# Transposing two operands by DMA instead of TensorE in a fused expert, scan, expert kernel

## The chip, the cores and the metric

One core of a Trainium2 chip runs the whole kernel. The time is the device time in microseconds (us) of that core for one execution, and what is given for a kernel is the median of its runs. The engines are TensorE (PE in the rows; PEld is its weight load), VectorE (DVE), ScalarE (ACT), GpSimd (POOL) and SyncE (SP). In this kernel SP only issues DMAs.

## The reference

Three layers run over x, 2 sequences of 2048 tokens by 1024 features. The first and the third are a feed-forward layer with 64 small experts of rank 16, of which each token takes four; the second is a selective scan over time with 16 states for each feature.

```python
def ffn(x, A, B, W, bias):
    vecs = einsum('arh,bsh->bsar', A, x)            # 64 experts x 16
    arrows = norm(vecs, axis=-1)
    _, idx = top_k(arrows, 4)
    routes = one_hot(idx, 64).sum(-2) / 4
    v = einsum('bsa,bsar->bsr', routes, vecs)
    delta = einsum('bsa,ajr,bsr->bsj', routes, B, v)
    return einsum('bsh,jh->bsj', x, W) + bias + delta

def scan(x, W_xproj, W_dt, b_dt, A_log, D_param):
    delta_r, B_mat, C_mat = split(einsum('btd,rd->btr', x, W_xproj))
    delta = softplus(einsum('btr,dr->btd', delta_r, W_dt) + b_dt)
    h = exp(delta * -exp(A_log)) * h + delta * B_mat * x     # step by step over t
    return sum(h * C_mat) + x * D_param

x = x + 0.5 * ffn(layernorm(x), ...)
x = x + scan(layernorm(x), ...)
x = x + 0.5 * ffn(layernorm(x), ...)
```

## The kernel before

**Units.** The 4096 tokens are 32 blocks of 128. Each block passes the feed-forward layer twice, so there are 64 *units* of work; a unit of kind 1 is a block's first pass, one of kind 2 its second. `plan` sets their order. The scan is cut into 256 *groups* of four 128x512 pieces (a group is 4 states of a feature tile over 512 tokens), and these groups, some five in a unit, are laid between the parts of units 5 to 57 (the *slots* of a unit). Units 0 to 4 and 58 to 63 have next to no scan work.

**Order.** There is no scheduler. Every engine has a function `unit(l, a, b)` written by hand; `a` is the current unit, `b` the next one, `l` the one before. Each engine goes through its own list in order and waits on semaphores. SP's list of DMAs is in order too: a wait for one DMA's source holds every later DMA back.

**One unit on TensorE** is, in this order: `base` (the product with W, 50 matmuls of 128x512 into `po`), between its parts the transposes and products of the scan's inputs (`scan_blocks`, `scan_products`, only behind a unit of kind 1), the transposes of the scan's result for a unit of kind 2 (`y_blocks`, f32, from `uT`, which is used as the landing place `auxy`), `z` (a matmul for the step sizes), then `routed_blocks` (16 transposes of the routed rows), `routed` (48 matmuls with B into `po`), with `norm_blocks` of the next unit between its last parts (8 f32 transposes of the normalised rows `xn`), and `experts` of the next unit (48 matmuls with A into `pv`). `states` sums scan pieces and lies in between.

**f16 pairs.** Each f32 operand is split into a high and a low f16 part. Products take high*high, high*low and low*high. `xT` and `uT` hold both parts of the transposed normalised rows and of the transposed routed rows.

**From experts to routed.** ScalarE squares `pv` into `sel` (`squares`), VectorE sums (`sums`), takes the four largest (`choose`) and writes the routed rows as f16 high and low part into the same `sel` (`gather`, L1004 and L1009, semaphore `s_u`). TensorE transposes them into PSUM (L553), ScalarE copies them into `uT` (`routed_copy`, L763), and `routed` may start.

**From normalising to experts.** VectorE takes mean and variance (`unit_stats`, L955 and L957), ScalarE refines the scale (`prepare`, nine tiny instructions) and writes `xn` (`normed`, L741), TensorE transposes in f32 into PSUM (L462), ScalarE copies the halves to the high part of `xT` (`high`, L746), VectorE subtracts for the low part (`low_part`, L978), and `experts` may start.

**The scan's feeding.** For each tile of 4 groups: `z` on TensorE (L615), softplus on ScalarE and VectorE (`magnitudes`, `softplus`, `delta`), a store to DRAM (`delta_out`, issued by ScalarE), and after it landed broadcasting loads on SP (`spread_inputs` L307, `spread_delta` L300). GpSimd multiplies with B (`times_b`, L425 and L430), ScalarE makes the decays (L825), VectorE scans (L1034), GpSimd multiplies with C (`times_c`, L438), TensorE sums (L628). `load_ranks` (L324) brings the ranks for eight `z`; before, it is issued with the first tile of the eight (`load_tile`). `store_tile` (L337) stores a finished tile.

## Time and profile before

| | |
|---|---|
| median of 3 runs | 3056.54 us (3044.06 to 3065.63) |
| the profiled execution's own time | 3055.02 us |
| its span, first to last instruction | 3053.2 us |
| granted TensorE clock, mean | 0.965 |
| busy | PE 90%, VectorE 75%, ScalarE 51%, GpSimd 77% |
| DMA | 340 MB, 111 GB/s mean |

The rows come from one profiled execution, 1.5 us under the median; the sums stand against 3055.0 us. Between span and own time lie 1.8 us. Times in rows are us from the start of the span. A timeline row gives start, duration, engine, line, operation, output and inputs, and in brackets the idle time of that engine just before and what ended it.

### The profile page before, as it was taken

The numbers are of one execution on the slowest core, as the hardware profiler recorded it, in microseconds if no ns is written. First come the engines' busy times: TensorE is split into PE (matmuls) and PEld (weight loads), VectorE is DVE, ScalarE is ACT, GpSimd is POOL, SyncE is SP. The second block draws the span as 40 slices with busy tenths as digits, with TensorE's granted clock in tenths as the row PEclk, the third lists the DMA queues.
The fourth block names the chain that finished last, engine by engine and source line by source line (L and its number), as shares of the span: only waits on it lengthen the run. The fifth ranks groups of instructions, "written<-read, shape, count | busy, mean of one in ns | idle before, by whom it ended". The sixth has DMA issues, their size and how long they took to land.

```text
span 3053.2 us, 41481 instructions
## 1 busy us (share of the span) xinstructions
PE 2742.9 (90%) x14592; PEld 1275.1 (42%) x14592; DVE 2289.5 (75%) x2915; ACT 1558.1 (51%) x2915; POOL 2348.7 (77%) x703
## 2 busy tenths in 40 slices
PE   5998998999899899889799898899889988988999
PEld 2554444444443344344344443444344433433444
DVE  8335888688778878887688787788787878888533
ACT  5335565565645456555546554554555545454321
POOL 2004998789889899898799798899898989889300
PEclk8999999999999999999999999999999999999999
DMA  5114432433344333433343234333343344333110
GB/s 196 44 44 135 124 119 92 135 120 120 112 135 133 110 110 106 145 105 105 119 150 118 86 109 140 129 98 125 118 137 99 110 130 129 118 114 111 49 42 35
DMA packets 174215, 340.05 MB, mean 111 GB/s; under 512 B 12979, under 2 KB 88883, under 8 KB 174006
## 3 DMA queue, kind: packets, MB, share of 16 engines
q1 hardware_dynamic: 157110, 303.83, 31.0%
q10 hardware_dynamic: 16896, 33.56, 3.6%
q8 instruction: 116, 1.90, 0.3%
q14 instruction: 93, 0.76, 0.1%
HBM read 234.05 MB, written 103.29 MB: 110 GB/s over the span
## 4 chain that ended last, share of the span: by engine, by line
PE 29%; DVE 23%; DMA 13%; ACT 9%; DVEq 9%; issue 7%; POOL 7%; SPq 1%; ACTq 1%; POOLq 0%
DVE mreg L1034 11%; PE po L470 9%; PE pv L470 7%; DMA delta_scratch<-mreg 6%; PE po L474 5%; PE pv L474 4%; ACT pA L825 3%; DMA yT_scratch<-mreg 3%; POOL mreg L430 3%; POOL mreg L438 3%; DVEq L1036 3%; DVE pv L1001 2%; DVE sel L1009 2%; DVEq L1000 1%; DVE sel L998 1%
## 5 line engine op out<-in xcount | busy, mean ns | idle before, releaser
L438 POOL TENSOR_TENSOR mreg<-mreg 128x2048 f32<-128x2048 f32 x256 | 1160.5, 4534 | 43.1 <-DVE hst L1037 42.7
L430 POOL TENSOR_TENSOR mreg<-mreg 128x1024 f32<-128x1024 f32 x340 | 794.8, 2361 | 349.5 <-DMA mreg<-delta_scratch 273.2
L825 ACT ACTIVATE pA<-mreg,nA 128x512 f32<-128x512 f32 x1024 | 696.4, 687 | 691.0 <-DVE mreg L1034 617.2
L1034 DVE TENSOR_TENSOR_SCAN mreg<-pA,hst,mreg 128x512 f32<-128x512 f32 x768 | 943.8, 1266 | 109.5 <-ACT pA L825 80.2
L470 PE MATMUL po<-wB,uT 128*128 128x512 f16 x2016 | 487.8, 392 | 44.2 <-ACT uT L763 44.1
L470 PE MATMUL po<-wW,xT 128*128 128x512 f16 x2016 | 464.4, 381 | 0.0
L470 PE MATMUL pv<-wA,xT 128*128 128x512 f16 x2016 | 458.6, 381 | 1.3 <-DVE xT L978 1.1
L425 POOL TENSOR_TENSOR mreg<-mreg 128x2048 f32<-128x2048 f32 x86 | 389.7, 4532 | 54.6 <-issue 54.6
L1034 DVE TENSOR_TENSOR_SCAN mreg<-pA,cst,mreg 128x512 f32<-128x512 f32 x256 | 314.9, 1267 | 38.8 <-ACT pA L825 35.5
L628 PE MATMUL py<-mreg,Em 128*32 128x512 f32 x2048 | 280.8, 621 | 63.1 <-DVE mreg L1046 34.1
L470 PEld LDWEIGHTS po<-wB,uT 128*128 128x128 f16 x2016 | 198.7, 101 | 287.6 <-ACT uT L763 51.8
L470 PEld LDWEIGHTS pv<-wA,xT 128*128 128x128 f16 x2016 | 193.6, 98 | 274.4 <-issue 36.2
L470 PEld LDWEIGHTS po<-wW,xT 128*128 128x128 f16 x2016 | 198.3, 98 | 235.3 <-issue 17.8
L474 PE MATMUL pv<-wA,xT 128*128 128x512 f16 x1008 | 241.8, 383 | 35.2 <-DVE xT L978 34.9
L982 DVE TENSOR_REDUCE n<-sel 128x32 f32<-128x512 f32 x128 | 87.3, 683 | 237.4 <-ACT sel L753 237.0
L474 PE MATMUL po<-wW,xT 128*128 128x512 f16 x1008 | 254.9, 399 | 0.0
L474 PE MATMUL po<-wB,uT 128*128 128x512 f16 x1008 | 238.1, 379 | 0.0
L1014 DVE SCALAR_TENSOR_TENSOR xin<-po,sc,xin 128x512 f32<-128x512 f32 x128 | 95.6, 747 | 158.8 <-PE po L474 154.8
L474 PEld LDWEIGHTS pv<-wA,xT 128*128 128x128 f16 x1008 | 97.3, 98 | 162.3 <-issue 51.1
L474 PEld LDWEIGHTS po<-wW,xT 128*128 128x128 f16 x1008 | 98.3, 102 | 152.1 <-issue 60.4
L753 ACT ACTIVATE sel<-pv 128x512 f32<-128x512 f32 x128 | 74.8, 585 | 168.7 <-PE pv L474 168.5
L474 PEld LDWEIGHTS po<-wB,uT 128*128 128x128 f16 x1008 | 98.6, 98 | 105.0
(128 smaller groups left out, 2745.0 us busy)
## 6 DMA issues: line engine op xcount, KB each, us to landing
mreg<-delta_scratch SPq DMA_DIRECT2D x256, 512.0 KB, 5.3
delta_scratch<-mreg ACTq DMA_DIRECT2D x128, 256.0 KB
xin<-x SPq DMA_DIRECT2D x32, 512.0 KB, 4.7
x_scratch<-xin SPq DMA_DIRECT2D x32, 512.0 KB, 7.2
xnT_scratch<-auxs SPq DMA_DIRECT2D x32, 512.0 KB, 2.7
mreg<-xnT_scratch SPq DMA_DIRECT2D x64, 256.0 KB, 4.2
mreg<-bc_scratch SPq DMA_DIRECT2D x64, 256.0 KB, 5.7
yT_scratch<-mreg SPq DMA_DIRECT2D x64, 256.0 KB, 6.7
```

The costliest lines, as they stand in the source:

```text
L425: pool.tensor_tensor(Hr[:, G % NH, :, :], u, b.broadcast_to([P, 4, CT]), ALU.mult).then_inc(s_bm, 2)
L430: pool.tensor_tensor(Hr[:, G % NH, 2 * h:2 * h + 2, :], u, b.broadcast_to([P, 2, CT]), ALU.mult).then_inc(s_bm, 1)
L438: pool.tensor_tensor(h, h, Cr[:, g, :].unsqueeze(1).broadcast_to([P, 4, CT]), ALU.mult).then_inc(s_cm, 1)
L470: last = nc.tensor.matmul(dst, lhs[:, 0, k, :], w[:, wb, k, nb * HF:(nb + 1) * HF], start=(first and k == 0 and wb == 0), stop=False)
L474: last = nc.tensor.matmul(dst, lhs[:, 1, k, :], w[:, 0, k, nb * HF:(nb + 1) * HF], start=False, stop=(stop and k == KD - 1))
L628: last = nc.tensor.matmul(py[32 * s:32 * s + 32, :], Em[:, :], Hr[:, G % NH, s, :], start=(g == 0), stop=(g == 3), tile_position=(0, 32 * s))
L753: nc.scalar.activation(sel[:, nb * HF:(nb + 1) * HF], pv[:, nb, :], ACT.Square).then_inc(s_sq, 1)
L825: nc.scalar.activation(pA[:, i % 2, :], Dr[:, 2 * (n % NPR) + i % 2, :], ACT.Exp, scale=nA[:, c:c + 1]).then_inc(s_dA, 1)
L982: V.tensor_reduce(n2[:, nb * NE // 2:(nb + 1) * NE // 2], sel3[:, nb * NE // 2:(nb + 1) * NE // 2, :], AX.X, ALU.add)
L1014: V.scalar_tensor_tensor(dst, po[:, nb, :], sc[:, 3:4], dst, ALU.mult, ALU.add).then_inc(s_res, 1)
L1034: V.tensor_tensor_scan(h, pA[:, i % 2, :], h, before, ALU.mult, ALU.add).then_inc(s_sc, 1)
L1036: dve.drain()
```

## The change

- TensorE no longer transposes the routed rows (`routed_blocks` is gone) nor the normalised rows (`norm_blocks` is gone). ScalarE's copies `routed_copy` and both half copies `high` from PSUM are gone, VectorE's two half subtractions too.
- ScalarE now rounds `xn` to f16 in token order into `sel` (`high`, one instruction of 128x1024), VectorE subtracts in one instruction of 128x1024 (`low_part`), both SBUF to SBUF.
- SP issues two DMA transposes of the routed rows (`turn`, `sel` to `uT`) and two of the normalised rows (`turn_rows`, `sel` to `xT`) in each unit, 128x1024 in f16 each, 256 KB. Each has a wait: for `s_u`; for `s_xhi`, `s_xlo`, and for the end of `base`, which still reads `xT` (`s_bd`, new). The first unit's `turn_rows` is issued by ScalarE.
- `sel` is used by both, so `high` waits for the routed rows' transposes to have landed.
- Places: `load_ranks` moves ahead by a part of a unit or more (`ranks_due`); `store_tile` stands ahead of the spreads; `z(a, 1)` comes one part of `routed` earlier, `states(a, 0)` one part of `base` later; `unit_stats` comes one scan later; `low_part` stands behind scan 12 as a whole; `delta(a, 1)` and `delta(a, 2)` are set among the last scans.

```diff
+        xh = sel[:, :].bitcast(f16).rearrange("p (c n) -> p c n", c=2)
...
+        def turn_rows(q, b):
+
+            for part in range(2):
+                q.wait_ge(s_xhi if part == 0 else s_xlo, b.u + 1)
+                if part == 0:
+                    q.wait_ge(s_bd, b.u)
+                q.dma_start_transpose(xT[:, part, :, :], xh[:, part, :]).then_inc(s_xT[part], 16)
...
+            def turn(a, y_done):
+
+                for part in range(2):
+                    sp.wait_ge(s_u, a.u * 2 + 1 + part)
+                    if part == 0:
+                        sp.wait_ge(s_yT, 2 * y_done)
+                    src = un2[:, part, :, :].rearrange("p k q -> p (k q)")
+                    sp.dma_start_transpose(uT[:, part, :, :], src).then_inc(s_uc[part], 16)
...
+            def ranks_due(a, pos):
+
+                if pos in a.zs and a.zs[pos] % KD == 0:
+                    load_ranks(a.zs[pos] // KD)
...
                 slot(a, 1)
+                turn(a, a.f2s + (b is not None and b.kind == 2))
                 slot(a, 2)
...
+                if b:
+                    turn_rows(sp, b)
                 slot(a, 3)
                 slot(a, 4)
...
             def experts(b, nb, third):
                 if nb == 0 and third != 1:
-                    pe.wait_ge(s_xhi, b.u * 2 + 2)
-                    pe.wait_ge(s_xlo, b.u * 2 + (1 if third == 0 else 2))
+                    pe.wait_ge(s_xT[third // 2], 16 * b.u + 16)
+                    pe.wait_ge(s_u, 2 * b.u)
...
                 if nb == 0 and third != 1:
-                    pe.wait_ge(s_uc, a.u * 2 + (1 if third == 0 else 2))
+                    pe.wait_ge(s_uc[third // 2], 16 * a.u + 16)
...
-                routed_blocks(a, 0)
+                routed(a, 0, 0)
                 states(a, 2)
+                routed(a, 0, 1)
                 if late:
                     pe.wait_ge(s_pc, late.w + 1)
-                routed_blocks(a, 1)
-                routed(a, 0, 0)
-                routed(a, 0, 1)
+                z(a, 1)
                 routed(a, 0, 2)
-                z(a, 1)
                 routed(a, 1, 0)
-                if b:
-                    norm_blocks(b, 0)
                 routed(a, 1, 1)
-                if b:
-                    norm_blocks(b, 1)
                 routed(a, 1, 2)
...
-            def high(b, half):
-                act.wait_ge(s_xT, b.u * 2 + 1 + half)
-                nc.scalar.activation(xT[:, 0, half * KB:(half + 1) * KB, :].rearrange("p k t -> p (k t)"), ptn[half],
-                                     ACT.Copy).then_inc(s_xhi, 1)
+            def high(b):
+                act.wait_ge(s_uc[0], 16 * b.u)
+                act.wait_ge(s_uc[1], 16 * b.u)
+                act.drain()
+                nc.scalar.activation(xh[:, 0, :], xn[:, :], ACT.Copy).then_inc(s_xhi, 1)
...
-            def low_part(b, half):
-                dve.wait_ge(s_xhi, b.u * 2 + 1 + half)
-                hi = xT[:, 0, half * KB:(half + 1) * KB, :].rearrange("p k t -> p (k t)")
-                lo = xT[:, 1, half * KB:(half + 1) * KB, :].rearrange("p k t -> p (k t)")
-                V.tensor_tensor(lo, ptn[half], hi, ALU.subtract).then_inc(s_xlo, 1)
+            def low_part(b):
+                dve.wait_ge(s_xhi, b.u + 1)
+                V.tensor_tensor(xh[:, 1, :], xn[:, :], xh[:, 0, :], ALU.subtract).then_inc(s_xlo, 1)
```

What stands in a row on TensorE at the routed product of a unit in the middle of the scan. Before:

```order
L553 MATMUL pt<-idh,sel 128x128 x8
L628 MATMUL py<-mreg,Em 32x512 x4
L553 MATMUL pv<-idh,sel 128x128 x8
L470 MATMUL po<-wB,uT 128x512 x16
L474 MATMUL po<-wB,uT 128x512 x8
L615 MATMUL pv<-mreg,wdt 128x512
L470 MATMUL po<-wB,uT 128x512 x8
L462 MATMUL pv<-idf,xn 128x128 x4
L470 MATMUL po<-wB,uT 128x512 x8
L462 MATMUL pt<-idf,xn 128x128 x4
L474 MATMUL po<-wB,uT 128x512 x8
```

The same place in the changed kernel (L498 and L502 are the products, L647 the sums, L634 is `z`):

```order
L498 MATMUL po<-wB,uT 128x512 x8
L647 MATMUL py<-mreg,Em 32x512 x4
L498 MATMUL po<-wB,uT 128x512 x8
L634 MATMUL pv<-mreg,wdt 128x512
L502 MATMUL po<-wB,uT 128x512 x8
L498 MATMUL po<-wB,uT 128x512 x16
L502 MATMUL po<-wB,uT 128x512 x8
```

Four rows of transposes are gone, `z` stands ahead of the product's low part, and a `states` lies between the first two parts of the product.

What stands in a row on VectorE from the statistics of the next unit (the rows of BN) to the second result, in the same unit. Before:

```order
L955 BN_STATS ln_st<-xin 128x6 x2
L957 BN_AGGR ln_mv<-ln_st 128x2
L1034 SCALAR_TENSOR_TENSOR mreg<-pA,hst,mreg 128x512 x3
L1037 TENSOR_REDUCE hst<-mreg 128x4
L1014 SCALAR_TENSOR_TENSOR xin<-po,sc,xin 128x512
L1034 SCALAR_TENSOR_TENSOR mreg<-pA,hst,mreg 128x512 x2
L978 TENSOR_TENSOR xT<-pv,xT 128x512
L1034 SCALAR_TENSOR_TENSOR mreg<-pA,hst,mreg 128x512 x2
L1037 TENSOR_REDUCE hst<-mreg 128x4
L1046 SCALAR_TENSOR_TENSOR mreg<-mreg,Dp,py 128x512
L1034 SCALAR_TENSOR_TENSOR mreg<-pA,hst,mreg 128x512
L978 TENSOR_TENSOR xT<-pt,xT 128x512
```

The same in the changed kernel (L974 is the one subtraction, L1030 a scan, L1010 a result):

```order
L953 BN_STATS ln_st<-xin 128x6 x2
L955 BN_AGGR ln_mv<-ln_st 128x2
L1030 SCALAR_TENSOR_TENSOR mreg<-pA,hst,mreg 128x512 x2
L1033 TENSOR_REDUCE hst<-mreg 128x4
L1010 SCALAR_TENSOR_TENSOR xin<-po,sc,xin 128x512
L1042 SCALAR_TENSOR_TENSOR mreg<-mreg,Dp,py 128x512
L1030 SCALAR_TENSOR_TENSOR mreg<-pA,hst,mreg 128x512
L974 TENSOR_TENSOR sel<-xn,sel 128x1024
L1030 SCALAR_TENSOR_TENSOR mreg<-pA,hst,mreg 128x512 x3
L1033 TENSOR_REDUCE hst<-mreg 128x4
L1010 SCALAR_TENSOR_TENSOR xin<-po,sc,xin 128x512
```

The low part is whole three scans behind the statistics; its second half stood eight scans behind them.

What stands in a row on SP in a unit whose spreads are in its last slot, in the changed kernel (`turn`, `turn_rows`, `store_tile`, the spreads of inputs and of step sizes, the early `load_ranks`, the result's store):

```order
L351 DMA_TRANSPOSE uT<-sel 128x8x128 x2
L244 DMA_TRANSPOSE xT<-sel 128x8x128 x2
L342 DMA yT_scratch<-mreg 128x4x128
L314 DMA mreg<-delta_scratch 128x1x1024 x2
L307 DMA mreg<-delta_scratch 128x1x1024
L331 DMA mreg<-delta_rank_scratch 128x4x128
L415 DMA x_scratch<-xin 128x1024
```

Before, such a unit's spreads had no transposes ahead of them, and the store of the tile stood behind them.

## Rows read from the trace of the kernel before

**Rows 1.** The page: busy time and share of the span of each engine.

```profile
PE 2742.9 (90%) x14592; PEld 1275.1 (42%) x14592; DVE 2289.5 (75%) x2915; ACT 1558.1 (51%) x2915; POOL 2348.7 (77%) x703
```

**Rows 2.** Busy time by stretch: units 1 to 4, the scan's units, the rest.

```profile
94.60:250.80 156.20, 153.15 (x843) 83.19 (x842) 54.95 (x89) 54.77 (x128) 0.00 (x0) 1.00 0.18 58
250.80:2849.20 2598.40, 2337.52 (x12506) 1073.08 (x12505) 2087.61 (x2613) 1408.89 (x2625) 2323.57 (x682) 0.96 0.37 118
2849.20:3053.20 204.00, 196.11 (x1020) 95.32 (x1018) 76.08 (x119) 42.06 (x88) 0.84 (x1) 1.00 0.11 38
```

**Rows 3.** Waits of GpSimd in the scan's stretch: total us, times, longest.

```profile
POOL mreg L430 <- DMA mreg<-delta_scratch: 91.5, 18, 9.1
POOL mreg L430 <- PE py L628: 76.2, 35, 6.8
POOL mreg L425 <- issue: 54.6, 21, 7.9
POOL mreg L438 <- DVE hst L1037: 42.7, 20, 4.5
```

**Rows 4.** Waits of TensorE in the scan's stretch, the same columns.

```profile
PE pt L462 <- DVE xin L964: 76.2, 27, 6.8
PE po L470 <- ACT uT L763: 38.0, 31, 2.9
PE pv L474 <- DVE xT L978: 34.9, 20, 5.0
...
PE pv L615 <- DMA mreg<-delta_rank_scratch: 33.7, 3, 14.1
```

**Rows 5.** Timeline of unit 61, behind the scan: TensorE, then VectorE.

```profile
2956.22 0.38 PE L547 MATMUL po<-brow,onesb 128*128 128x512 bf16 x1
...
2967.92 0.61 PE L553 MATMUL pt<-idh,sel 128*128 128x128 f16 x8
...
2969.64 3.63 PE L470 MATMUL po<-wB,uT 128*128 128x512 f16 x16 [0.67 <-ACT uT L763]
...
2976.56 0.60 PE L462 MATMUL pv<-idf,xn 128*128 128x128 f32 x4
2977.00 1.89 PE L470 MATMUL po<-wB,uT 128*128 128x512 f16 x8
...
2991.25 0.38 PE L547 MATMUL po<-brow,onesb 128*128 128x512 bf16 x1
...
2962.25 1.21 DVE L1004 SCALAR_TENSOR_TENSOR sel<-mask,pv 128x1024 f16<-128x1024 f32 x1
```

**Rows 6.** Timeline of unit 36, in the scan: TensorE, then VectorE, then ScalarE.

```profile
1779.39 0.39 PE L547 MATMUL po<-brow,onesb 128*128 128x512 bf16 x1
...
1797.34 0.62 PE L553 MATMUL pt<-idh,sel 128*128 128x128 f16 x8
...
1813.33 3.63 PE L470 MATMUL pv<-wA,xT 128*128 128x512 f16 x16
...
1825.68 0.39 PE L547 MATMUL po<-brow,onesb 128*128 128x512 bf16 x1
...
1786.29 1.21 DVE L1004 SCALAR_TENSOR_TENSOR sel<-mask,pv 128x1024 f16<-128x1024 f32 x1
...
1806.06 1.24 ACT L741 ACTIVATE xn<-xin,ln_nm,ln_r 128x1024 f32<-128x1024 f32 x1
```

**Rows 7.** The page: ScalarE's copies of the routed rows.

```profile
L763 ACT ACTIVATE uT<-pv 128x1024 f16<-128x1024 f16 x64 | 65.3, 1020 | 15.5 <-issue 8.4 <-PE pv L553 7.1
```

**Rows 8.** DMA issues in 250:2850: count, KB, median us to landing; last, L282.

```profile
mreg<-xnT_scratch SPq DMA_DIRECT2D x63, 256.0 KB, 4.3
...
uT<-yT_scratch SPq DMA_DIRECT2D x28, 512.0 KB, 5.9
...
DMA to landing us min/median/max: 3.2/5.6/10.9
```

**Rows 9.** SP's longest wait, and one of its issues in unit 36.

```profile
SPq L307 <- DMA delta_scratch<-mreg: 766.7, 52, 32.3
...
1782.61 9.02 SPq L307 DMA_DIRECT2D mreg<-delta_scratch  x2
```

More of the change, by code:

```diff
@@ L216, in build @@
         s_mv = sem("s_mv"); s_xn = sem("s_xn")
[L217 removed]
+        s_xT = [sem(f"s_xT{n}") for n in range(2)]; s_bd = sem("s_bd"); s_xhi = sem("s_xhi"); s_xlo = sem("s_xlo")
         s_vec = sem("s_vec"); s_sq = sem("s_sq"); s_n2 = sem("s_n2"); s_mk = sem("s_mk"); s_gm = sem("s_gm")
[L219 removed]
+        s_u = sem("s_u"); s_uc = [sem(f"s_uc{n}") for n in range(2)]
         s_out = sem("s_out"); s_res = sem("s_res")
@@ L327, in load_tile @@
                 q, k = t // KD, t % KD
-                if k == 0:
-                    load_ranks(q)
                 sp.wait_ge(s_stn, 16 * (4 * q + 4))
@@ L344, in slot @@
                 if G % 4 == 2:
+                    if t >= 2:
+                        store_tile(t - 2)
                     if t < NGRP // 4:
@@ L348, in slot @@
                         spread_delta(t, 0)
-                    if t >= 2:
-                        store_tile(t - 2)
                 if G % 4 == 3 and t < NGRP // 4:
@@ L476, in product @@
                 return last
-            def norm_blocks(b, half):
-                if half == 0:
-                    pe.wait_ge(s_xn, b.u + 1)
-                pe.wait_ge(s_uc, max(b.u * 2 - half, 0))
-                blocks(ptn[half], lambda k: xn[:, (half * KB + k) * P:(half * KB + k + 1) * P], s_xT, idf[:, :])
             def y_blocks(b, half):
@@ L547, in base @@
                     nc.tensor.matmul(po[:, nb, :], onesb[:, :], brow[:, nb * HF:(nb + 1) * HF], start=True, stop=False)
-                product(po[:, nb, :], xT, wW, nb, third, False, False)
-            def routed_blocks(a, part):
-                pe.wait_ge(s_u, a.u * 2 + 1 + part)
-                for k in range(KD):
-                    last = nc.tensor.transpose(pth[part][:, k * P:(k + 1) * P], un2[:, part, k, :], idh[:, :])
-                last.then_inc(s_uT, 1)
+                last = product(po[:, nb, :], xT, wW, nb, third, False, False)
+                if nb == 1 and third == 2:
+                    last.then_inc(s_bd, 1)
             def first_routed(a):
-                pe.wait_ge(s_uc, a.u * 2 + 2)
+                pe.wait_ge(s_uc[0], 16)
+                pe.wait_ge(s_uc[1], 16)
                 for k in range(KD):
@@ L859, in unit @@
                 delta_copy(a, 0)
-                routed_copy(a, 0, a.f2s + (b is not None and b.kind == 2))
                 decays(10, 11)
                 delta_out(a, 0)
-                routed_copy(a, 1, 0)
-                if a.u == 0:
-                    weights_b(6, KD)
                 decays(11, 12)
@@ L870, in unit @@
                     normed(b, 2 * (a.f1s - (a.kind == 1)))
+                if b:
+                    high(b)
                 decays(12, 14)
@@ L897, in _ @@
             normed(US[0], 0)
-            high(US[0], 0)
-            high(US[0], 1)
+            high(US[0])
+            turn_rows(act, US[0])
             act.wait_ge(s_scl, 1)
@@ L1072, in unit @@
                 delta(a, 0)
-                scans(8, 9)
+                scans(8, 10)
                 if b:
                     unit_stats(b)
-                scans(9, 12)
+                scans(10, 12)
                 result(a, 0)
-                scans(12, 14)
+                scans(12, 13)
                 if b:
-                    low_part(b, 0)
-                scans(14, 17)
+                    low_part(b)
+                scans(13, 16)
                 delta(a, 1)
-                if b:
-                    low_part(b, 1)
+                scans(16, 17)
                 result(a, 1)
-                delta(a, 2)
                 if a.kind == 1:
@@ L1090, in unit @@
                     stats("ln2", xin[:, a.p, :], s_mv2)
-                scans(17, 20)
+                scans(17, 19)
+                delta(a, 2)
+                scans(19, 20)
                 if b:
```

50 lines of the change are left out of this document (19 added, 31 removed).

## The prediction

> **What bounds the kernel now.** The page's busy shares come first [rows 1]. TensorE is busy nine tenths of the span, which invites the thought that all work taken from it is time won. The busy times by stretch say where that holds [rows 2]. I cut the span where unit 1, unit 5 and unit 58 begin. In the 156 us of units 1 to 4 and the 204 us from unit 58 on, TensorE is busy 98% and 96%, and GpSimd has nothing to do: there TensorE is the bound, with one proviso that unit 61 shows below. In the 2598 us between, 53 units of 49.0 us, TensorE is busy 2338 us and GpSimd 2324 us. Two engines at 90% of one stretch can't both be its bound. GpSimd's work alone is 2323.6 / 53 = 43.8 us a unit, a floor that this change doesn't move.
>
> The waits tell what lies on top. GpSimd waits 265 us there [rows 3]: 92 for the spread step sizes, 76 for TensorE to free a buffer, 55 with no named releaser at the same kind of instruction (`times_b`, which also waits for that buffer), 43 for VectorE's scans. TensorE waits too [rows 4]: 76 us for VectorE's additions between the two halves of `y_blocks`, 38 for ScalarE's copies of the routed rows, 35 for VectorE's low part, 34 in three places for the ranks.
>
> Then one unit of the scan, followed on three engines [rows 6]. Unit 36 starts `base` at 1779.4. The first routed rows are ready at 1787.5 (1786.29 + 1.21), TensorE asks for them at 1797.3, 9.8 us later. The normalised rows of the next unit are ready at 1807.3 (1806.06 + 1.24), and `experts` starts at 1813.3, 6.0 us behind them, with the transposes and copies in between. The next `base` starts at 1825.7, 12.4 us behind that. This is a ring: experts, choice, scans in VectorE's order, statistics, `xn`, transposed rows, experts. The routed side has room in it, the normalised side has none. So **what takes the place of the last 6.0 us decides the 53 units of the scan**, more than TensorE's busy time does.
>
> **The unknown.** Call L the time from the moment a transposing DMA may be issued until TensorE can use what it wrote, SP's issue, landing and semaphore included. No DMA of before transposes or goes from SBUF to SBUF. The nearest rows are plain ones [rows 8]: loads of 256 KB, the same bytes, land in 4.3 us (median), loads of 512 KB into `uT` itself in 5.9 in the scan, and that line's fastest and slowest took 3.2 and 10.9. Upper reason: SP can stall in an issue (9.0 us for two, [rows 9]), and a transpose may need more and smaller pieces. Lower reason: no DRAM is read. I take **L = 5.2**, between the two medians, nearer the upper since the same tile is written, and keep 3.2 and 10.9 as ends.
>
> **The change part by part.**
>
> *TensorE outside the scan.* In unit 61 the routed transposes and the wait for the copy fill 2967.92 to 2969.64, 1.72 us, and four f32 transposes fill 2976.56 to 2977.00, 0.44 us, twice a unit [rows 5]. That is 2.6 us a unit. The proviso: the first routed rows are ready at 2963.46 (2962.25 + 1.21), and TensorE wants them at 2967.92, so 4.5 us are free and a wait of L - 4.5 = 0.7 us comes. The normalised side has room there: ScalarE loses two copies of 1.02 us [rows 7] ahead of `xn`. Unit 61 ends 1.9 us sooner. Six such units give 11 us. Units 1 to 4 have more `base` work ahead and keep the whole 2.6: 10 us. Together **-22 us** (rounded up for the ends of the stretch).
>
> *The ring in the scan.* Gone are the f32 transposes and half copies. New is `high`, the shape of the `xn` write, so 1.24 us [rows 6], then L. `xn` itself comes sooner: the two routed copies are off ScalarE (up to 2.0 us), but the statistics stand a scan later and the scans pace ScalarE; by where ScalarE stands in unit 36 I get 0.5, and take 1.0 as the mean of all units. So `experts` starts at 1807.3 - 1.0 + 1.24 + L instead of 1813.3, a shift of **L - 5.8 us a unit**; for L = 5.2 that is -0.6, and 53 units give **-32 us**. What else TensorE sheds there (16 + 8 transposes, the 38 us of waits for the copies) shortens stretches in which it would now wait for `xT`; it is off the path, and it pays only if L is short. If L falls below some 4, GpSimd's 43.8 us and its own waits catch up.
>
> *The low part.* Its second half stood behind four more scans and a `delta`, and TensorE waited 34.9 us for it in 20 units [rows 4]. Now it is one instruction (1.21 us, the shape of L1004 in [rows 6]) three scans behind the statistics, and its transposed form is wanted only 3.5 us (16 matmuls) after the high one. I count the **-35 us** whole. VectorE's work falls by nothing that matters.
>
> *The ranks.* `load_ranks` leaves its place behind spreads that wait for DRAM; the three waits of 33.7 us hold the longest single stall of TensorE in the scan (14.1 us). I count **-34 us**. If the load is still late in one, 14 come back.
>
> *The routed side in the scan.* `turn` stands behind slots 0 and 1. Where these hold spreads (two units in five), SP may still wait for the step sizes of the last unit to land (767 us in all, [rows 9]), and the transposes queue behind 1.5 MB. The room is 9.8 us, less L = 5.2: covered by 4.6 us. I cost it at nothing; with a late SP it costs what goes beyond.
>
> *SP's list.* Four more issues a unit, and three waits. Behind `turn_rows` stand the spreads of slots 3 and 4, some 21 units of the 53. GpSimd already waits 91.5 us for spreads [rows 3], so delay there is not covered. `turn_rows` becomes free at about the time at which such spreads are issued now, and one ScalarE copy less brings the step sizes to DRAM 1.0 us sooner. I net it to nothing, with +2 us in 21 units, +42 us, as its upper bound. `z(a, 1)` a part earlier, and `store_tile` ahead of the spreads, go the same way: nothing, within that bound.
>
> *The first unit.* `experts` of unit 0 waits for the weights; the transposes land in that time.
>
> **The sum**: 3055.0 - 22 - 32 - 35 - 34 = 2932 us, 4.0% less. The profiled time stands 1.5 us under the median, which is nothing here.
>
> **What the notes say of L.** Behind the rows: the Trainium skill gives 1309 ns for a 128x128 block by DMA against 390 ns by TensorE ("VectorE: DVE Perf Modes", The three transpose paths). As an estimate from that page, eight blocks one after another would be 10.5 us, near the upper end of the range, and the sum some 3270 us. Another page of the Trainium skill calls transposing DMAs on this chip as fast as regular ones ("Advanced Engine Details and Errata", X-Bar Transpose (TRN2)), which would be the 256 KB row, and 2870 us. No run so far shows which holds.
>
> **The rivals.**
>
> *Late transposes, slower (0.25).* The DMAs go at the pace of the slowest plain ones. Per us of L above 5.2 the scan loses 53 us and the ends 10. The gain of 123 is used up at L = 5.2 + 123/63 = 7.2, and it is slower from there: at L = 8.5, 53 x 2.7 - 69 + 10 x 1.4 = +88, so 3143 us; at 10.9, 53 x 5.1 - 69 + 10 x 3.8 = +239, so 3294. For it: slowest landing and SP's 9.0 us issues, a ring without slack, two of the pieces in a row in one queue. Against: DMA engines are busy only 37% in the scan [rows 2], and medians are 4.3 and 5.9.
>
> *Fast transposes (0.21).* L = 4.2, the plain 256 KB landing. 53 x -1.6 = -85, the two waits -69, the ends 10 x -2.6 = -26: 2875 us. It needs GpSimd's waits for TensorE to vanish as well (131 us by [rows 3], which allows it). For: no DRAM. Against: GpSimd's waits for spreads stay, and set in as soon as the ring is shorter.
>
> *The gain is eaten on SP (0.14).* L between 6.5 and 7.2, or L as forecast with late spreads (+42) and a rank load still late: 3025 to 3085 us, no change that can be told. For: SP's 767 us of waits in one ordered list. Against: most of them lie where nothing waits for SP.
>
> **How the numbers follow.** My forecast, L from 4.5 to 6.5, is the likeliest at 0.40, and its own range is 2890 to 3015. Fast 0.21, eaten 0.14, slower 0.25. A change of 1% is about what measuring this kernel can tell from none. Faster by over 1% (under 3025) takes the forecast and the fast case: 0.61; within 1% 0.14; slower 0.25. The range goes from a little under the fast case, 2860, to L = 8.5, 3145; some 0.06 lie below and 0.13 above.
>
> **What would show it.** The issues' table gives the landing of `uT<-sel` and `xT<-sel`: about 4 us from issue, and nothing near 8. TensorE's waits should name the `xT` DMA at the start of `experts`, 1 to 2 us a unit, and hardly the `uT` DMA in the scan; its waits for the low part and the ranks should be gone, and its busy time down by some 200 us while the span falls by only 123. Units behind the scan should take 33 us instead of 35.0 (2956.22 to 2991.25, [rows 5]). GpSimd's waits for spreads should stay near 91 us. I am wrong if the transposes take 8 us or more, or hold SP so long that spreads are late; or, on the good side, if other orders on ScalarE let `xn` come much sooner than 1 us.

## The result, and the profile after

| | before | after |
|---|---|---|
| median | 3057.51 us (3044.06 to 3065.63, 4 runs) | 3155.32 us (3148.72 to 3164.22, 4 runs) |
| ratio, 95% interval | | 1.0326 [1.0278, 1.0374], slower |
| profiled execution, its span | 3055.02, 3053.2 us | 3160.56, 3158.8 us |

The forecast was 2932 us, the range 2860 to 3145. The time lies 10 us above the range.

The page after, busy times and packets, against [rows 1]:

```profile
PE 2682.7 (85%) x13056; PEld 1160.7 (37%) x13056; DVE 2374.4 (75%) x2851; ACT 1451.1 (46%) x2723; POOL 2373.4 (75%) x703
DMA packets 444539, 406.99 MB, mean 129 GB/s; under 512 B 283315, under 2 KB 359219, under 8 KB 444342
```

TensorE is 60 us less busy, of 200 forecast, and ScalarE 107. VectorE, with 64 instructions fewer, is 85 us *more* busy, and GpSimd, with the same 703, is 25 us more busy. Then the table of DMA issues (tiles, queue, count, median us to landing), for the new DMAs:

```profile
uT<-sel SPq DMA_TRANSPOSE x128, 3.3
xT<-sel SPq DMA_TRANSPOSE x126, 3.1
xT<-sel ACTq DMA_TRANSPOSE x2, 18.9
```

The median transpose lands in 3.1 to 3.3 us, at the *lower* end of what the prediction allowed. Yet the kernel is slower, and the median hides eleven slow ones in the scan, shown below. The waits of TensorE and GpSimd in the scan's stretch (us in total, times, longest), against [rows 3, 4]:

```profile
POOL mreg L458 <- PE py L647: 127.0, 46, 10.2
PE pv L498 <- DMA xT<-sel: 103.6, 27, 10.0
PE po L498 <- DMA uT<-sel: 97.3, 25, 7.1
PE pv L502 <- DMA xT<-sel: 40.8, 21, 7.9
```

242 us of waits for transposed rows stand where 38 and 35 stood. The wait for the low part (L502 after, L474 before) was to vanish and is 40.8 us in place of 34.9. From the starts of `base`: unit 1 starts at 104.4 in place of 94.6 (+10 us); units 1 to 4 take 39.1 us each on average in both; the 53 units of the scan take 50.95 in place of 49.03 (+102 us); units 58 to 62 take 34.6 in place of 35.5 (-5 us). That is the 106 us between the spans. The scan carries the loss. Its 1.9 us a unit divide so, on average: from the start of `base` to the end of `xn` 0.2 us less, from there to the start of `experts` 1.2 us more, from there to the next `base` 0.9 us more.

**The subtraction.** By line (busy, mean ns of one), after:

```profile
L974 DVE TENSOR_TENSOR sel<-xn,sel 128x1024 f16<-128x1024 f32 x64 | 180.7, 2824 | 7.5 <-ACT sel L759 7.5
```

and before, where one operand was PSUM:

```profile
L978 DVE TENSOR_TENSOR xT<-pv,xT 128x512 f16<-128x512 f32 x64 | 44.3, 692 | 64.2 <-ACT xT L746 64.2
L978 DVE TENSOR_TENSOR xT<-pt,xT 128x512 f16<-128x512 f32 x64 | 43.4, 678 | 13.2 <-ACT xT L746 13.2
```

The sum asked 1.21 us for the new one. It takes 2.82 on average (3.2 in the scan) and up to 9.6. The timeline of the slowest, after (VectorE, then GpSimd, TensorE, SP):

```profile
2937.06 9.61 DVE L974 TENSOR_TENSOR sel<-xn,sel 128x1024 f16<-128x1024 f32 x1
2946.59 3.62 DVE L1030 TENSOR_TENSOR_SCAN mreg<-pA,hst,mreg 128x512 f32<-128x512 f32 x3
...
2936.48 4.66 POOL L458 TENSOR_TENSOR mreg<-mreg 128x1024 f32<-128x1024 f32 x2
2941.09 4.50 POOL L466 TENSOR_TENSOR mreg<-mreg 128x2048 f32<-128x2048 f32 x1
...
2938.32 3.63 PE L498 MATMUL pv<-wA,xT 128*128 128x512 f16 x16
2949.84 3.60 PE L502 MATMUL pv<-wA,xT 128*128 128x512 f16 x8 [7.90 <-DMA xT<-sel]
...
2935.18 12.75 SPq L244 DMA_TRANSPOSE xT<-sel  x2
```

It stands through three multiplications of GpSimd and ends 1.08 us after the last (2946.67 against 2945.59). SP waits with it, and TensorE waits 7.9 us. By their starts and ends, 22 of the 64 subtractions take 1.20 to 1.24 us; each of the other 42 ends 1.08 or 1.09 us after a GpSimd multiplication ends. Eleven of the 22 lie outside the scan, where GpSimd has no such work. The harm goes both ways (unit 27, GpSimd, then VectorE):

```profile
1416.51 4.53 POOL L453 TENSOR_TENSOR mreg<-mreg 128x2048 f32<-128x2048 f32 x1
1421.01 5.49 POOL L466 TENSOR_TENSOR mreg<-mreg 128x2048 f32<-128x2048 f32 x1
...
1420.62 1.50 DVE L974 TENSOR_TENSOR sel<-xn,sel 128x1024 f16<-128x1024 f32 x1
```

The subtraction gets in at 1421.04, where the first multiplication ends, and the next takes 5.49 us in place of 4.53. Seventeen other multiplications of this line grew to 5.5 us in the same way.

**The routed rows.** The timeline of unit 31 after (SP, then TensorE):

```profile
1602.22 0.37 SPq L342 DMA_DIRECT2D yT_scratch<-mreg  x1
1602.69 1.17 SPq L314 DMA_DIRECT2D mreg<-delta_scratch  x2
1605.93 5.86 SPq L351 DMA_TRANSPOSE uT<-sel  x2
...
1613.06 3.57 PE L498 MATMUL po<-wB,uT 128*128 128x512 f16 x8 [6.33 <-DMA uT<-sel]
```

The first rows were ready at 1597.3. SP stood at a tile's store, then issued that tile's spreads, and issued the rows' transpose 8.6 us after they were ready. Over the scan, by starts of rows, the issue comes 5.2 us behind the rows on average and `routed` starts 11.7 behind them, where 9.8 of room was counted in unit 36. Forty of the 53 issues are over 1 us late, and they have two causes. Nineteen stand right behind another DMA in SP's list. The other 21 follow within 0.6 us of the last transpose that TensorE makes out of `uT`: `turn` also waits until the scan's result, which landed in `uT`, has been read (`s_yT`).

**Eleven units.** Every fourth or fifth unit of the scan (5, 10, 15, 20, 25, 30, 34, 39, 44, 49, 54) has three spreads of 512 KB and a few smaller DMAs right ahead of `turn_rows` in SP's list. Unit 10 (SP, then TensorE); the high part was ready at 543.5:

```profile
545.35 1.17 SPq L314 DMA_DIRECT2D mreg<-delta_scratch  x2
546.62 0.56 SPq L307 DMA_DIRECT2D mreg<-delta_scratch  x1
...
550.32 4.91 SPq L244 DMA_TRANSPOSE xT<-sel  x2
...
556.45 5.08 PE L498 MATMUL pv<-wA,xT 128*128 128x512 f16 x16 [9.98 <-DMA xT<-sel]
```

In these eleven the high part's transpose is issued 3.4 to 6.8 us late and then takes 7.1 us on average to land, 11.7 in all; in the other 42 it is 3.3 in all. TensorE stands 78.9 of its 103.6 us for `xT` in the eleven, and in each of them the subtraction took only 1.20 to 1.23 us. So this wait isn't the subtraction's.

**The first unit** (TensorE): its transposes, issued by ScalarE, took 18.9 us to land among the loads of weights.

```profile
27.39 3.77 PE L520 MATMUL pv<-wA,xT 128*128 128x512 f16 x10 [27.39 <-DMA xT<-sel]
```

### The profile page after: what moved, and what is told of

It reads as the page before. It is cut to its first block, busy times and chain, and to the rows that moved or that the text cites. A ratio compares the mean times of both kernels' runs of the same rounds, so it can differ in the third digit from the quotient of the medians.

```text
span 3158.8 us, 38460 instructions
## 1 busy us (share of the span) xinstructions
PE 2682.7 (85%) x13056; PEld 1160.7 (37%) x13056; DVE 2374.4 (75%) x2851; ACT 1451.1 (46%) x2723; POOL 2373.4 (75%) x703
## 4 chain that ended last, share of the span: by engine, by line
DVE 29%; PE 22%; DMA 16%; DVEq 11%; ACT 7%; issue 7%; SPq 3%; POOL 3%; ACTq 2%; POOLq 0%
DVE mreg L1030 13%; PE po L498 7%; PE pv L498 6%; DMA delta_scratch<-mreg 5%; DVE sel L974 4%; DMA uT<-sel 4%; DVEq L1032 3%; DMA xT<-sel 3%; PE po L502 3%; PE pv L502 3%; DVE pv L997 3%; ACT pA L829 2%; DMA xin<-x_scratch 2%; DVEq L996 2%; DVE sel L1005 2%
## 5 line engine op out<-in xcount | busy, mean ns | idle before, releaser
L466 POOL TENSOR_TENSOR mreg<-mreg 128x2048 f32<-128x2048 f32 x256 | 1176.5, 4596 | 25.9 <-DVE hst L1033 25.9
L458 POOL TENSOR_TENSOR mreg<-mreg 128x1024 f32<-128x1024 f32 x340 | 799.8, 2373 | 444.1 <-DMA mreg<-delta_scratch 317.0
L1030 DVE TENSOR_TENSOR_SCAN mreg<-pA,hst,mreg 128x512 f32<-128x512 f32 x768 | 940.5, 1264 | 107.9 <-ACT pA L829 107.6
L498 PE MATMUL pv<-wA,xT 128*128 128x512 f16 x2016 | 493.5, 401 | 126.4 <-DMA xT<-sel 118.5
L498 PE MATMUL po<-wB,uT 128*128 128x512 f16 x2016 | 493.4, 396 | 104.8 <-DMA uT<-sel 104.8
L498 PE MATMUL po<-wW,xT 128*128 128x512 f16 x2016 | 464.8, 381 | 0.0
L453 POOL TENSOR_TENSOR mreg<-mreg 128x2048 f32<-128x2048 f32 x86 | 389.6, 4531 | 59.9 <-issue 59.6
L498 PEld LDWEIGHTS pv<-wA,xT 128*128 128x128 f16 x2016 | 201.0, 103 | 431.4 <-DMA xT<-sel 151.2
L498 PEld LDWEIGHTS po<-wB,uT 128*128 128x128 f16 x2016 | 194.4, 101 | 434.9 <-issue 230.4
L1030 DVE TENSOR_TENSOR_SCAN mreg<-pA,cst,mreg 128x512 f32<-128x512 f32 x256 | 313.7, 1264 | 42.4 <-ACT pA L829 39.7
L647 PE MATMUL py<-mreg,Em 128*32 128x512 f32 x2048 | 290.7, 641 | 26.4 <-POOL mreg L466 25.7
L498 PEld LDWEIGHTS po<-wW,xT 128*128 128x128 f16 x2016 | 198.8, 99 | 237.3 <-issue 21.6
L502 PE MATMUL pv<-wA,xT 128*128 128x512 f16 x1008 | 244.7, 387 | 40.9 <-DMA xT<-sel 40.8
L1010 DVE SCALAR_TENSOR_TENSOR xin<-po,sc,xin 128x512 f32<-128x512 f32 x128 | 94.7, 740 | 231.5 <-PE po L502 228.3
L502 PE MATMUL po<-wW,xT 128*128 128x512 f16 x1008 | 252.7, 396 | 0.0
L502 PE MATMUL po<-wB,uT 128*128 128x512 f16 x1008 | 238.1, 379 | 0.0
L974 DVE TENSOR_TENSOR sel<-xn,sel 128x1024 f16<-128x1024 f32 x64 | 180.7, 2824 | 7.5 <-ACT sel L759 7.5
L502 PEld LDWEIGHTS pv<-wA,xT 128*128 128x128 f16 x1008 | 97.9, 99 | 169.8 <-DMA xT<-sel 53.5
L502 PEld LDWEIGHTS po<-wB,uT 128*128 128x128 f16 x1008 | 98.7, 98 | 128.2 <-issue 15.7
```

Of the source, the lines that this page charges most:

```text
L453: pool.tensor_tensor(Hr[:, G % NH, :, :], u, b.broadcast_to([P, 4, CT]), ALU.mult).then_inc(s_bm, 2)
L458: pool.tensor_tensor(Hr[:, G % NH, 2 * h:2 * h + 2, :], u, b.broadcast_to([P, 2, CT]), ALU.mult).then_inc(s_bm, 1)
L466: pool.tensor_tensor(h, h, Cr[:, g, :].unsqueeze(1).broadcast_to([P, 4, CT]), ALU.mult).then_inc(s_cm, 1)
L498: last = nc.tensor.matmul(dst, lhs[:, 0, k, :], w[:, wb, k, nb * HF:(nb + 1) * HF], start=(first and k == 0 and wb == 0), stop=False)
L502: last = nc.tensor.matmul(dst, lhs[:, 1, k, :], w[:, 0, k, nb * HF:(nb + 1) * HF], start=False, stop=(stop and k == KD - 1))
L647: last = nc.tensor.matmul(py[32 * s:32 * s + 32, :], Em[:, :], Hr[:, G % NH, s, :], start=(g == 0), stop=(g == 3), tile_position=(0, 32 * s))
```

## The experiments

All ratios are to the kernel before on the same chip; "points" are hundredths of it, 30.5 us each. Intervals reach 0.1 to 0.5 points to each side, so a difference between two rows is good to some 0.3 to 0.6 points. "All on TensorE" means the transposes of both sides as before the change.

| run | routed rows | normalised rows | order on SP | median us | ratio |
|---|---|---|---|---|---|
| after | DMA | DMA, SBUF subtraction | as changed | 3155.32 | 1.0326 |
| x1 | TensorE | TensorE | before, ranks early | 3032.72 | 0.9917 [0.9886, 0.9949] |
| x5 | TensorE | TensorE | as changed | 2987.08 | 0.9791 [0.9757, 0.9825] |
| x9 | TensorE | TensorE | store late | 3009.74 | 0.9854 [0.9832, 0.9876] |
| x4 | DMA | TensorE | as changed | 3025.59 | 0.9897 [0.9872, 0.9923] |
| x11 | DMA | TensorE | `turn` early | 2958.32 | 0.9688 [0.9668, 0.9709] |
| x15 | DMA | TensorE | `turn` earlier yet | 2955.52 | 0.9698 [0.9683, 0.9712] |
| x6 | DMA | TensorE | `turn` early, store late | 2983.94 | 0.9775 [0.9744, 0.9806] |
| x10 | TensorE | DMA, PSUM subtraction | as changed | 3018.54 | 0.9882 [0.9863, 0.9902] |
| x2 | DMA | DMA, PSUM subtraction | as changed | 3080.50 | 1.0078 [1.0052, 1.0104] |
| x7 | DMA | DMA, SBUF, halves | as changed | 3273.14 | 1.0725 [1.0694, 1.0756] |
| x14 | DMA | DMA, PSUM subtraction | `turn` early | 3021.74 | 0.9903 [0.9872, 0.9934] |
| x8 | DMA | DMA, PSUM subtraction | `turn` early, store late | 3067.72 | 1.0047 [1.0029, 1.0065] |
| x12 | DMA | DMA, PSUM subtraction | x8, rows ahead of spreads | 3181.90 | 1.0433 [1.0404, 1.0461] |
| x13 | DMA | DMA, SBUF subtraction | `turn` early | 3125.50 | 1.0251 [1.0208, 1.0293] |
| x3 | DMA | DMA by ScalarE's queue | as changed | 3270.52 | 1.0695 [1.0656, 1.0733] |

**First: which part loses.** x1 is the kernel before with `load_ranks` alone in its new place:

```diff
-                if k == 0:
-                    load_ranks(q)
+                if b:
+                    ranks_due(b, 0)
```

> The kernel before with one part of the change alone: load_ranks is issued early (ranks_due), nothing else. If the three long waits for the ranks (33.7 us) sit on the path, as my forecast had it, this takes 25 to 34 us off 3057, about 3027. If something else is late next in those units, less than 10 us.

Measured 0.9917: 25 us won, of the 34 forecast. x4 puts the normalised side back on TensorE (`norm_blocks`, `high` and `low_part` in halves), the routed side stays with DMA, all places new:

```diff
-                if b:
-                    turn_rows(sp, b)
...
+                if b:
+                    norm_blocks(b, 0)
                 routed(a, 1, 1)
+                if b:
+                    norm_blocks(b, 1)
```

> The changed kernel with the normalised rows' side put back as it was (f32 transposes on TensorE, half copies, half subtractions from PSUM); only the routed rows go by DMA. If the normalised side holds the whole loss, as the forecast's ring says, this is below the kernel before, 2990 to 3040. If the late issue of the routed transposes (105 us of TensorE's waits for uT) holds it, it stays above 3100.

Measured 0.9897, 4.3 points under the changed kernel: the normalised side holds more than the whole loss. x5 also puts the routed side back (`routed_blocks`, `routed_copy`), so that only the new places are left:

> All transposes on TensorE as before, but the changed kernel's other places (early ranks, the store ahead of the spreads, the moved z, states, statistics, scans and delta). x4 (routed rows by DMA, these places) stands at 3026, early ranks alone at 3033. If the routed rows by DMA are what x4 gains, this is slower than x4 by some 20 us or more; if the places gain it, this is at 3020 to 3035 and DMA on the routed side is worth nothing.

Measured 0.9791: the places alone win 64 us, 25 of them the ranks. From there the routed side by DMA, as placed, costs 1.1 points. So both sides lose against the same places, and the places hid a part of it. By starts of `base`, the changed kernel loses 81 us to x5 in the eleven units and 95 us in the other 42 of the scan.

**Second: the subtraction.** x2 takes one operand of it from PSUM. ScalarE makes the high part straight from `xin` and then writes the f32 rows into two PSUM tiles that are free there; `experts` waits for the subtraction (this wait frees PSUM):

```diff
-                V.tensor_tensor(xh[:, 1, :], xn[:, :], xh[:, 0, :], ALU.subtract).then_inc(s_xlo, 1)
+                for half in range(2):
+                    part = slice(half * HF, (half + 1) * HF)
+                    last = V.tensor_tensor(xh[:, 1, part], ptn[half], xh[:, 0, part], ALU.subtract)
+                last.then_inc(s_xlo, 1)
...
+                    pe.wait_ge(s_xlo, b.u + 1)
```

> The changed kernel, but ScalarE makes the high part straight from the input rows and writes the f32 normalised rows into PSUM, so that VectorE's subtraction has one operand from PSUM and one from SBUF, in two halves. Theory A (VectorE's one subtraction with both operands in SBUF is held up beside GpSimd, 3.2 us instead of 1.2 in the scan, up to 5.6): it returns to 2 x 0.7 us, the waits for the low part of xT (41 us) go, and with the high part 1.2 us earlier the kernel gains 60 to 110 us, to about 3070. Theory B (SP's order and the landing decide, the subtraction is hidden): under 25 us gained, 3130 to 3155.

x2 differs from the changed kernel in four things (operand, a high part made one ScalarE instruction sooner, halves, and the wait of `experts`). x7 is its control: the same order, halves and wait, and only `ptn[half]` is `xn[:, part]` in SBUF.

> The control for x2: the same order and the same halves (high part straight from the input rows, then the f32 rows, then two subtractions), but the f32 rows lie in SBUF, not in PSUM. Theory A (the subtraction is held up by GpSimd because both its operands are in SBUF): most of x2's gain of 75 us is gone, about 3130. If x2 gained by the earlier high part alone: about 3080 as x2.

1.0078 against 1.0725, 6.5 points or some 197 us for where one operand lies (with the waits that guard `xn` or the PSUM tiles). The subtractions by line, x2:

```profile
L979 DVE TENSOR_TENSOR sel<-pt,sel 128x512 f16<-128x512 f32 x64 | 43.6, 681 | 0.0
L979 DVE TENSOR_TENSOR sel<-pv,sel 128x512 f16<-128x512 f32 x64 | 42.9, 670 | 8.7 <-ACT pt L760 8.7
```

and x7:

```profile
L980 DVE TENSOR_TENSOR sel<-xn,sel 128x512 f16<-128x512 f32 x128 | 266.3, 2120 | 8.9 <-ACT xn L761 8.9
```

675 ns from PSUM, 2120 from SBUF. This settles the operand as the cause of the long subtraction. x7 stands 4 points above the changed kernel. Two reasons fit and were not tried apart: it can be caught twice a unit, and `experts` waits for the whole low part at its start. In x7 by line:

```profile
L498 PE MATMUL pv<-wA,xT 128*128 128x512 f16 x2016 | 535.3, 426 | 282.3 <-DVE sel L980 180.4 <-DMA xT<-sel 97.4 <-ACT mreg L815 4.4
```

So 6.5 points are the price under that wait, which x2 has too (33.9 us for L979 there). For the changed kernel itself the nearest figure is x2's gain, 2.5 points or 76 us. It is the net of all four differences, and no run takes the subtraction's share out of it.

**Third: who issues the normalised rows' transposes.** x3 has ScalarE issue them, which writes the high part and needs no signal from itself:

```diff
-                    turn_rows(sp, b)
...
+                    turn_rows(act, b, (0,))
                 decays(12, 14)
                 magnitudes(a, 1)
                 decays(14, 15)
+                if b:
+                    turn_rows(act, b, (1,))
```

> The changed kernel with the two transposes of the normalised rows issued by ScalarE instead of SP: the first right behind the high part, the second three decays later. Theory B (they are late since they stand in SP's list behind waits and behind 1.5 MB of spreads): the delay from the high part to the issue, mean 0.97 us in the scan and 3 to 7 us in the ten units with two tiles, goes to nothing, gain 30 to 60 us, to about 3110. Theory A (the low part is the late one): under 20 us, and ScalarE's two issues of 1.3 us may eat that, 3140 to 3170.

A miss: 1.0695. ScalarE's list is in order too, and the second issue waits for the slow subtraction, with decays behind it. From x3's timeline (VectorE, then ScalarE), and its waits:

```profile
1738.26 4.81 DVE L976 TENSOR_TENSOR sel<-xn,sel 128x1024 f16<-128x1024 f32 x1
...
1743.10 1.26 ACTq L244 DMA_TRANSPOSE xT<-sel  x1
1744.46 0.69 ACT L827 ACTIVATE pA<-mreg,nA 128x512 f32<-128x512 f32 x1 [5.33 <-DVE mreg L1032]
```

```profile
PE pv L500 <- DMA xT<-sel: 206.0, 45, 11.2
```

ScalarE stands 5.3 us (the named releaser, a scan, had long ended; the issue ahead of the decay was late), the scans get their decays late (VectorE waits 261.5 us for them in place of 147.3), and TensorE's 40.8 us for the low part became 206. In the eleven units, where SP's list was the trouble, x3 is 27 us faster than the changed kernel; in the other 42 it is 135 us slower. The wait for the low part did not leave with SP; it went to an engine on which more depends.

**Fourth: SP's order.** x6 makes two moves on x4: `turn` ahead of slot 1, and `store_tile` behind the spreads again.

```diff
-                slot(a, 1)
                 turn(a, a.f2s + (b is not None and b.kind == 2))
+                slot(a, 1)
```

> x4 with SP's list changed: the routed rows' transposes ahead of slot 1, and the store of a finished tile behind the spreads, as before. In x4 SP issues the transpose 5.1 us after the rows are ready (mean in the scan) and TensorE waits 125 us for uT. If that delay is on the path, 20 to 50 us go, to about 2990. If VectorE or GpSimd close the gap, or the spreads of slot 1 come late instead, it stays at 3015 to 3035.

x8 makes the same two on x2:

> x2 with SP's list changed as in x6. What is left of x2's loss (3080 against 3053) should then be SP's: if so, it comes to 3030 to 3050. If spreads are later, it is 3080 or more.

0.9775 from 0.9897, as expected, but only 1.0047 from 1.0078, between the two cases of x8. To part the two moves, x9 is x5 with the store behind the spreads, and x11 is x4 with the early `turn` alone.

> x5 (all transposes on TensorE, new places, 2987) with the store of a finished tile behind the spreads again. If the store ahead of the spreads delays the spreads (SP waits 871 us for it in x5, against 79 before), this gains 10 to 30 us, to about 2965. If it is free there, 2980 to 2995.

> x4 with the routed transposes ahead of slot 1 alone, the store left ahead of the spreads. x6 gained 42 us by both moves. If the earlier transposes do it, this is 2980 to 2990; if the store does it, 3020 to 3030.

x9 loses 0.6 points to x5, so the early store, which I had costed at nothing, is worth 19 us there, which fits neither of x9's cases. Two other pairs agree: x11 is 0.9 points under x6, and x14 (below) 1.4 under x8. x11 went below both its cases; it is the best kernel of the study up to there, 0.9688. TensorE's waits for the routed rows, x4 and then x11:

```profile
PE po L488 <- DMA uT<-sel: 125.4, 38, 9.6
```

```profile
PE po L488 <- DMA uT<-sel: 20.2, 20, 2.3
```

Early enough, the routed transposes by DMA win 1.0 point over TensorE's (x11 against x5); one slot later they lose 1.1. The move takes only the list's part of the delay: in x11 the issue is still 3.2 us late on average, in 27 of 29 late units because of the wait for TensorE's reads of `uT`:

```profile
SPq L341 <- PE pt L480: 368.5, 32, 19.7
```

x10 is the other single side: routed rows on TensorE, normalised rows by DMA with the PSUM subtraction.

> The missing corner: only the normalised rows by DMA (with the subtraction from PSUM as in x2), the routed rows on TensorE as before, new places. Reference is x5 at 2987. If the two sides add, this is 3080 - (3026 - 2987) = 3040. If SP's list is the trouble only when both sides use it, 2990 to 3010.

Measured 0.9882, 0.9 points over x5: this side loses even with a quick subtraction. It lies between its two cases, and the two sides together (x2) cost 0.9 points more than their sum. By starts of `base`, x10 loses 62 us to x5 in the eleven units and *wins* 32 us in the other 42. x12 asks whether the place of `turn_rows` behind the spreads is why. It is x8 with them ahead:

```diff
+                if b:
+                    turn_rows(sp, b)
                 slot(a, 2)
-                if b:
-                    turn_rows(sp, b)
                 slot(a, 3)
```

> x8 (3068) with the transposes of the normalised rows ahead of slot 2's spreads. If their queueing behind the spreads is what x8 still loses, 3030 to 3050; if the spreads, now held by the wait for the normalised rows, are worth more, 3090 or above.

Worse by 3.9 points. Waits of x8 and then of x12, whole span (GpSimd's has a first wait of about 180 us in every kernel):

```profile
PE pv L499 <- DMA xT<-sel: 138.2, 15, 13.2
POOL mreg L459 <- DMA mreg<-delta_scratch: 292.2, 41, 176.5
```

```profile
POOL mreg L459 <- DMA mreg<-delta_scratch: 389.5, 43, 181.8
PE pv L499 <- DMA xT<-sel: 3.2, 1, 3.2
```

TensorE's 135 us are gone, and GpSimd gets 97 more: with SP standing at `turn_rows` until ScalarE has made the rows, the spreads are late. One ordered queue serves two consumers, and one of them waits. x12 moves `turn_rows` in every unit; a move in the eleven alone was not tried.

**Last: do the two losses add?** x13 is the changed kernel with `turn` ahead of slot 1, x14 the same move on x2, x15 is x11 with `turn` further ahead, right behind `load_x`.

> The changed kernel with one move: turn (the routed transposes) is issued ahead of slot 1 on SP. Theory that SP's place for the routed rows and the two-SBUF-operand subtraction are separate losses that add: this run gains what x11 gained over x4, about 68 us, so about 3090 us (3075 to 3110), and the waits of TensorE for uT fall from 105 us to under 40. Rival, that the late low part is what TensorE waits for whatever the routed rows do: under 20 us is gained, 3135 to 3160 us.

> x2 (f32 rows in PSUM, high part straight from xin, subtraction in halves) with turn ahead of slot 1 and the late store left ahead. If the two losses add: 3080 less 68, about 3012 us; the normalised side by DMA then still costs about 50 us over x11. Rival, that with the rows late SP's earlier turn only shifts the wait to xT: 3050 to 3080 us.

> x11 with turn still earlier, right behind load_x and ahead of the late store. If the wait for the routed rows is already gone in x11, nothing is left to gain and the store goes later: 2955 to 2970 us. If rows are still late in x11: 2935 to 2950 us.

In the changed kernel they do not add: the early `turn` wins 0.75 points (give or take 0.6), which fits neither case of x13. It wins 1.75 in x2, so that x14 comes within 10 us of the forecast for losses that add, and 2.1 in x4. The waits of x13, from an execution 18 us faster than its median:

```profile
PE pv L498 <- DMA xT<-sel: 120.1, 29, 10.4
PE pv L502 <- DMA xT<-sel: 72.4, 25, 10.7
PE po L498 <- DMA uT<-sel: 20.0, 19, 2.7
```

The wait for `uT` falls from 105 us (whole span) to 20, and 32 of the 85 come back as a longer wait for the low part: TensorE arrives sooner at rows that the subtraction still holds. The other way round, x2's edit wins 2.5 points with a late `turn` and 3.5 with an early one. x14, with both, is 4.2 points under the changed kernel, where the single gains sum to 3.2. Against x5, x14 wins 42 us in the 42 units and still loses 77 us in the eleven. x15 is level with x11: with 20 us of waits left in it, nothing remains to be had there. No version beats x11 and x15.

## Why the prediction was wrong

Three terms of the sum failed, all in the scan: the low part, booked as a gain of 35 us; the routed side, booked at nothing; and SP's list, booked at nothing. With them the ring's term of -32 us turned into a loss. What each measured stands below, after the one unknown that it named.

**The transposes' time, L.** One number was taken for what was two distributions. The median issue to landing is 3.1 to 3.3 us, and the median issue takes SP 1.24 to 1.32 us; in unit 33 of the changed kernel, issue to first use on TensorE is 3.1 us (1721.27 to 1724.39). But L was defined from the moment a transpose may be issued. So measured, in the scan, it is 5.0 us on average for the normalised rows, close to the forecast's 5.2, made of 3.3 in 42 units and 11.7 in eleven. For the routed rows it is 9.8: 5.2 until the issue and 4.6 to land. The Trainium skill has two figures for the landing. Eight blocks one after another, estimated from the Trainium skill ("VectorE: DVE Perf Modes", The three transpose paths) at 10.5 us, are not what the trace shows. "As fast as regular" (the Trainium skill, "Advanced Engine Details and Errata", X-Bar Transpose (TRN2)) agrees in the median, 3.1 to 3.3 against 4.3 for a plain load of the same bytes [rows 8]. The prediction's 2870 us for that case should be 2880 by its own sum.

**"The low part ... is one instruction (1.21 us ...) three scans behind the statistics. I count the -35 us whole."** This step failed. The row used for 1.21 us (L1004, [rows 6]) reads a PSUM tile; the new subtraction reads two SBUF tiles. Shown: 2.82 us on average, 1.22 where GpSimd is idle, 675 against 2120 ns in x2 and x7. The wait that was to vanish stayed, 40.8 us for 34.9. x2's edit, of which the quick subtraction is one of four parts, is worth 2.5 points (76 us), 3.5 with `turn` early. By starts of `base`, all of the 87 us between x13 and x14 in the scan lie in the 42 units where the subtraction was held up, and none in the eleven. "VectorE's work falls by nothing that matters" was wrong by 85 us upward. A rule was there to be read: the Trainium skill ("SBUF — State Buffer", Who interferes with whom) says that a VectorE instruction with two SBUF inputs contends with a GpSimd instruction that reads SBUF, and that the loser is blocked for the other's whole instruction. The trace agrees: 42 subtractions end 1.08 us behind the end of a GpSimd multiplication, none in between; three of them waited longer than one such instruction. By that rule a wait of half a multiplication (4.53 us) in most units was to be priced; I had no rival for it.

**"The routed side ... covered by 4.6 us. I cost it at nothing."** This step failed too. I took L = 5.2, which was to hold SP's issue, and left SP's wait out of it; the issue alone is 5.2 us late on average (unit 31: 8.6), and the whole is 9.8. The wait for `s_yT` was in the diff and in no term. The two losses share a ring, so 23 us are won back by moving `turn` alone, 53 with the subtraction mended, 64 with the normalised side on TensorE. The view that would have told it is the SP timeline of several units, two-tile ones too; I read one.

**"SP's list ... net to nothing."** The third step that failed. The parts were missed on both sides: the early store wins 19 us (x9 against x5), and `turn_rows` costs. GpSimd's waits for spreads rise from 273.2 to 317.0 us, 44 us where +42 was kept as a bound. What no term held is the other direction, spreads that hold up the transposes: the eleven units, with 78.9 us of TensorE's waits. x12 shows that one place further ahead in the list is worse. With a PSUM operand, the normalised side by DMA still costs 0.9 points (x10 against x5), 2.1 beside an early `turn` (x14 against x11). The unit times put the whole of that loss inside the scan into the eleven units; no run mends these alone.

**TensorE's busy time** fell by 60 us, not some 200. The 1536 transposes were busy for at most 159 us (84 on L553 and 75 on L462, by their groups before), so 200 was too much from the start. And the matmuls that are left take longer: `pv<-wA,xT` 401 ns on average after (L498 on the page), 381 before (L470 by line), at a granted clock of 0.94 in the scan's stretch in place of 0.96 [rows 2]. TensorE pauses oftener there. That it is the waits that lower the clock was not tried apart.

**The ring.** The claim "what takes the place of the last 6.0 us decides the 53 units" held: the loss is in those units, while TensorE's busy time fell. "`xn` comes 1.0 sooner" was 0.2 (its end is 29.4 us behind the start of `base` in place of 29.6). From the end of `xn` to `experts` it is 8.2 us in place of 7.1 on average; unit 36, which the sum used, had 6.0. From `experts` to the next `base` it is 13.1 in place of 12.1.

**The ends.** Behind the scan 0.9 us a unit were won, of 1.9: TensorE waits 0.7 to 1.7 us for `uT` there, where 0.7 was worked out, since SP issues 3.5 us behind the rows, mostly for the wait on `s_yT`. Units 1 to 3 take 36.0 us each in place of 38.8, a little more than the 2.6 forecast. Unit 4 gives it all back, 48.5 us in place of 39.7: the first spreads of the scan stand ahead of `turn_rows` in SP's list there, and TensorE waits 9.6 us for `xT`. "The transposes land in that time" for unit 0 was wrong: the first `experts` starts 6.1 us late (27.4 in place of 21.3), and unit 1 starts 10 us late.

**Ranks**: -25 of -34. **The other places**: 39 us more, which I put at nothing, measured with all transposes on TensorE (x5 against x1). In the changed kernel they hid some of the loss.

The rival "late transposes, slower" had the right side and in part the cause: transposes that wait in SP's list and land slowly behind other loads, in eleven units at 11.7 us, not DMAs that are slow by themselves (3.1 in the median). Nothing in its chance of 0.25 was for the subtraction.

## What to carry to other kernels

An instruction that replaces another of the same shape has its duration only if its operands lie in the same memories: before a VectorE operation with two SBUF operands is set beside a busy GpSimd, add a wait for that engine's instruction (2 us on average here, 8.4 at most). A DMA that replaces engine work has two prices, its landing and the delay until it can be issued, from its place in the queue's order and from its buffers; for the routed rows here the second was the larger. Look at its delay unit by unit: a median of 3.1 us hid eleven units of 11.7. When two losses lie on one ring, mending one shows only part of its worth, so undo them together as well as singly.

## What the runs showed of the hardware

- A DMA transpose of a 128x1024 f16 tile (256 KB), SBUF to SBUF, lands in 3.1 to 3.3 us in the median and holds SP 1.24 to 1.32 us in the issue. Behind three spreads of 512 KB it took 7.1 us to land (mean of eleven, up to 8.6). 256 of them add 270,000 packets under 512 B (12,979 before).
- Loads landed later after the change, but not for the transposes: the median of `mreg<-xnT_scratch` is 4.2 us before and 6.9 after, and it is 6.8 in x5, which has no transposing DMA, and 3.9 in x9, which is x5 with the store late.
- VectorE's wait for GpSimd can be longer than one GpSimd instruction: 9.61 us through three in a row. Where the subtraction got in ahead of a 128x2048 multiplication of L466, that one took 5.5 us in place of 4.5, 18 times.
- Queued from ScalarE among loads of weights at the start, the same transposes took 18.9 us (median of two).
